# Causal masking moved from a matrix product to GpSimd and step rows, the V bias folded into the output bias, the order laid out anew

## The chip, the cores and the metric

One Trainium2 chip; the kernel runs on one of its cores. A core has TensorE (PE in the profile; PEld is its weight loads), VectorE (DVE), ScalarE (ACT), GpSimd (POOL) and the DMA queues, here issued by SyncE (SP). Times are device microseconds of one launch.

## The reference

Sixteen sequences of 512 positions and width 256 pass six residual steps: an FFN whose inputs and weights are rounded blockwise to FP4, a Mamba block (a scan over 512 positions), the FFN again, a LoRA mixture, causal attention with ALiBi, and the LoRA mixture again. The change touches the attention:

```
def _L1_attn_ref(x, Wq, bq, Wk, bk, Wv, bv, Wo, bo):
    B, S, D, H = (2, 512, 256, 16)
    HD = D // H
...
    v = (x @ Wv + bv).reshape(Bb, Ss, H, HD)
    scores = jnp.einsum('bthd,bshd->bhts', q, k) / jnp.sqrt(jnp.asarray(HD, x.dtype))
    alibi = _alibi_bias(Ss, Ss, x.dtype)
    causal = jnp.triu(jnp.ones((Ss, Ss), bool), 1)
    scores = scores + alibi[None]
    scores = jnp.where(causal[None, None], -jnp.inf, scores)
    attn = jax.nn.softmax(scores, axis=-1)
    out = jnp.einsum('bhts,bshd->bthd', attn, v).reshape(Bb, Ss, Dd)
    return out @ Wo + bo
```

## The kernel before

One sequence is one round (rounds are counted from 0). From one round's first `va` write to the next it is some 274 us (round 4 at 1857.7, round 5 at 2130.8). Four threads of work are woven into each other: the FFNs and the head of the Mamba block (`first`), the scan (`second`), LoRA, attention and LoRA (`third`), and the norms ahead of them (`ahead`). They work on different sequences at the same time. Each engine has one queue of instructions in program order. What stands next to what is set by tables of numbers (`PE_PLAN`, `DVE_PLAN`, `ACT_PLAN`, `POOL_PLAN`, `SP_PLAN`, one dictionary for each thread): each step of a thread yields a time of its own, the table replaces it by a due time, and `weave` emits the steps in order of due time. A table changes the order alone, never how long anything takes.

Scan: 16 steps a sequence, each in two halves. For each half DVE multiplies the input into a PSUM tile `u` (L1557), scans it with the decay into `state` (L1562), and POOL multiplies `state` by C (L728) so that PE can sum it (L1174). POOL's product of a half waits for the `u` of the half behind it. `state` has three slots, and a slot is loaded again when PE has summed it.

FFN: four tiles a sequence, twice. Tanh on ScalarE, products and rounding on DVE (L1474, L1477, L1373 to L1387), a rescaling on POOL (L712), transposes and products on PE (L1092, L1112, L1118).

Attention: 16 heads in four sets j of four heads g, 512 positions in four tiles t. Phase `s` computes scores with queries on the partitions (L1270), adds a mask on the diagonal block by a product of an identity with `mask_q` (L1275), and DVE takes the maxima (L1650). Phase `e` computes the scores again with keys on the partitions, less the maxima (L1272), adds `mask_k` in the same way (L1275), and ScalarE writes exponentials into `pt` (L979), one unit at a time: four units for t = 0 and t = 1, two for t = 2, one for t = 3, 11 a set. Scores go to the PSUM banks `pg` and `pu` in turn. Then the value products (L1295) multiply each head's part of `pt` with `va`, which has a column of ones for the sum. `pt` holds two groups (j, t). On PE the value products of a group stand behind the scores of the next group (`after_group`). `va` is written by DVE, product plus bias (L1612), from `pd` and `pg`.

## Time and profile before

| | |
|---|---|
| Median of 3 runs | 4930.08 us (4922.24 to 6492.46) |
| The profiled execution | 4930.1 us, of which the span is 4928.3 |
| Busy, share of the span | PE 80%, DVE 81%, ACT 48%, POOL 32% |
| Mean granted clock of TensorE | 0.89 |
| Instructions | 52598, of these 17452 matmuls and 1035 on POOL |

Busy shares are means over a start, a steady stretch and a tail with different limits. An idle time is put down to what came last before the instruction started. Matmul ends are modelled; the distance from one start to the next shows what a matmul takes of PE when others stand behind it.

### The profile page before, as it was taken

The numbers are of one execution on the slowest core, as the hardware profiler recorded it, in microseconds if no ns is written. First come the engines' busy times: TensorE is split into PE (matmuls) and PEld (weight loads), VectorE is DVE, ScalarE is ACT, GpSimd is POOL, SyncE is SP. The second block draws the span as 40 slices with busy tenths as digits, with TensorE's granted clock in tenths as the row PEclk, the third lists the DMA queues.
The fourth block names the chain that finished last, engine by engine and source line by source line (L and its number), as shares of the span: only waits on it lengthen the run. The fifth ranks groups of instructions, "written<-read, shape, count | busy, mean of one in ns | idle before, by whom it ended". The sixth has DMA issues, their size and how long they took to land.

```text
span 4928.3 us, 52598 instructions
## 1 busy us (share of the span) xinstructions
PE 3918.3 (80%) x17452; PEld 1986.8 (40%) x17452; DVE 3998.4 (81%) x5964; ACT 2373.6 (48%) x4341; POOL 1599.9 (32%) x1035
## 2 busy tenths in 40 slices
PE   4556678887879888888989888888889798786868
PEld 2212334443535353444435353434435353334343
DVE  6588889898989989898989899898989899683412
ACT  2334344655555554645555554546555555443322
POOL 0143433333333333333333333333333333332000
PEclk8677889998989999998989899999989999797866
DMA  1487667767686777777677777777676867772100
GB/s 56 118 180 174 154 170 174 186 153 182 152 180 171 161 176 169 178 170 176 158 181 174 156 178 158 177 174 190 154 178 152 181 166 164 180 160 61 38 28 22
DMA packets 241427, 753.30 MB, mean 153 GB/s; under 512 B 37650, under 2 KB 132659, under 8 KB 171524
## 3 DMA queue, kind: packets, MB, share of 16 engines
q1 hardware_dynamic: 241156, 749.95, 64.7%
q8 instruction: 138, 2.26, 0.2%
q14 instruction: 133, 1.09, 0.1%
HBM read 647.30 MB, written 101.71 MB: 152 GB/s over the span
## 4 chain that ended last, share of the span: by engine, by line
PE 46%; DVE 26%; ACT 11%; DMA 9%; issue 5%; SPq 2%; POOL 2%; DVEq 0%; ACTq 0%; POOLq 0%
PE m L1118 6%; DVE state L1562 6%; DMA state<-dtx_scratch 5%; PE m L1092 5%; DVE mt L1650 5%; DVE u L1557 3%; PE y L1174 3%; PE m L1131 2%; PE y L1184 2%; PE pd L1295 2%; DMA decay<-dt_scratch 2%; ACT shared L979 2%; DVE front L1474 1%; PE pd L1210 1%; DVE front L1477 1%
## 5 line engine op out<-in xcount | busy, mean ns | idle before, releaser
L728 POOL TENSOR_TENSOR state<-state,bc 128x1024 f32<-128x1024 f32 x512 | 1216.0, 2376 | 1786.1 <-DVE u L1557 1786.1
L1562 DVE TENSOR_TENSOR_SCAN state<-decay,u 128x1024 f32<-128x1024 f32 x512 | 1169.1, 2283 | 13.8 <-ACT decay L909 1.8
L909 ACT ACTIVATE decay<-decay,a_neg 128x511 f32<-128x511 f32 x1024 | 671.1, 712 | 280.4 <-DMA decay<-dt_scratch 280.2
L1092 PE MATMUL m<-w_gu,hats_m 128*128 128x480 f32 (+1 forms) x1536 | 722.8, 604 | 38.7 <-DVE front L1477 31.3
L1557 DVE TENSOR_TENSOR u<-state,bc 128x1024 f32<-128x1024 f32 x512 | 632.8, 1236 | 85.5 <-DMA state<-dtx_scratch 74.9
L712 POOL TENSOR_TENSOR front<-front,hsc_m 128x704 f32<-128x704 f32 x128 | 206.1, 1610 | 797.1 <-DVE front L1387 797.1
L1118 PE MATMUL m<-w_dn,front 128*128 128x256 f32 (+1 forms) x1536 | 419.4, 418 | 42.6 <-ACT front L846 42.2
L1092 PEld LDWEIGHTS m<-w_gu,hats_m 128*128 128x128 f32 x1536 | 298.4, 205 | 303.0 <-issue 225.8
L1174 PE MATMUL y<-state,sel 128*32 128x512 f32 x2048 | 307.4, 676 | 132.2 <-POOL state L728 130.9
L1131 PE MATMUL m<-hats_m,w_in 128*128 128x512 f32 x512 | 292.0, 712 | 145.4 <-DVE front L1516 92.8
L1118 PEld LDWEIGHTS m<-w_dn,front 128*128 128x128 f32 (+1 forms) x1536 | 289.1, 201 | 164.7 <-ACT front L846 85.7
L827 ACT ACTIVATE front<-m 128x240 f32<-128x240 f32 (+1 forms) x384 | 137.0, 361 | 307.2 <-PE m L1092 281.7
L1650 DVE TENSOR_REDUCE mt<-pu 128x1 f32<-128x384 f32 (+3 forms) x368 | 235.1, 639 | 42.3 <-PE pu L1275 38.9
L1650 DVE TENSOR_REDUCE mt<-pg 128x1 f32<-128x384 f32 (+3 forms) x336 | 212.8, 633 | 48.2 <-PE pg L1275 47.4
L979 ACT ACTIVATE shared<-pg 128x512 f32<-128x512 f32 (+1 forms) x384 | 215.1, 560 | 59.8 <-PE pg L1275 58.3
L850 ACT ACTIVATE xx<-m 128x256 f32<-128x256 f32 x128 | 49.1, 383 | 374.8 <-PE m L1119 374.8
L1131 PEld LDWEIGHTS m<-hats_m,w_in 128*128 128x128 f32 x512 | 105.7, 223 | 298.2 <-DVE front L1516 113.9
L979 ACT ACTIVATE shared<-pu 128x512 f32<-128x512 f32 (+1 forms) x320 | 177.3, 554 | 91.3 <-PE pu L1275 87.6
L1474 DVE SCALAR_TENSOR_TENSOR front<-front,m 128x240 f32<-128x240 f32 (+1 forms) x384 | 149.1, 388 | 66.6 <-ACT front L827 66.6
L1295 PE MATMUL pd<-shared,va 128*17 128x512 f32 (+3 forms) x2048 | 199.8, 459 | 1.9
L693 POOL TENSOR_SCALAR less_r<-mv_r 128x4 f32<-128x4 f32 x48 | 13.5, 282 | 560.9 <-DVE mv_r L1438 560.9
L1272 PE MATMUL pg<-shared,kh 105*128 105x128 bf16 (+3 forms) x640 | 147.7, 297 | 57.4 <-ACT shared L979 48.0
(259 smaller groups left out, 7051.8 us busy)
## 6 DMA issues: line engine op xcount, KB each, us to landing
decay<-dt_scratch SPq DMA_DIRECT2D x256, 1024.0 KB, 7.4
state<-dtx_scratch SPq DMA_DIRECT2D x256, 1024.0 KB, 11.6
qk_scratch<-shared SPq DMA_DIRECT2D x64, 384.0 KB, 3.1
shared<-qk_scratch SPq DMA_DIRECT2D x384, 64.0 KB
kh<-qk_scratch SPq DMA_DIRECT2D x384, 64.0 KB
xs_scratch<-front SPq DMA_DIRECT2D x16, 1024.0 KB, 5.8
dt_scratch<-front SPq DMA_DIRECT2D x256, 64.0 KB, 2.7
dtx_scratch<-hats_m SPq DMA_DIRECT2D x256, 64.0 KB, 1.9
```

Source lines behind the costliest of these rows:

```text
L712: eng.tensor_tensor(blocks(f.hq[:, t % 2, :]), blocks(f.xn[:, 0:I]), spread(f.hsc[:, t % 2, :], I // QB), ALU.mult).then_inc(f.pool.sem, f ...
L728: eng.tensor_tensor(st, st, bc[:, 1:2, :].to_broadcast([P, WIDE, L]), ALU.mult).then_inc(scan_pool.sem, scan_pool.step(f"c{r}{h}"))
L909: ins = eng.activation(d, d, ACT.Exp, scale=a_neg[:, g:g + 1])
L979: eng.activation(pt[:, slot:slot + n, 0:width], heads(f"e{j}{t}{g}", width, n), ACT.Exp).then_inc(att_act.sem, att_act.step(f"e{j}{t}{g}"))
L1092: mm = eng.matmul(f.bank(f"gu{t}{p}")[:, 0:2 * width], norm.hat_t[:, k, t * P:(t + 1) * P], w_gu[:, k, 2 * lo:2 * (lo + width)], start=(k ...
L1118: eng.matmul(down[:, 0:D], f.h_t[0:rows, m, :], w_dn[0:rows, m, :], start=(m == 0), stop=False)
L1131: mm = eng.matmul(bank[:, :], w_in[:, k, m * P:(m + 1) * P], norm.hat_t[:, k, :], start=(k == 0), stop=(k == KD - 1))
L1174: mm = eng.matmul(Y[32 * j:32 * (j + 1), :], sel[:, r % Q, :], state[:, slot, j * L:(j + 1) * L], start=False, stop=(r % Q == Q - 1), skip ...
L1295: eng.matmul(PD[32 * g:32 * g + HD + 1, t * P:L], va[:, t, j * G + g, :], pt[:, (t * G + g) % NPT, 0:L - t * P], start=(t == 0), stop=True ...
L1557: eng.tensor_tensor(u[:, :].rearrange("p (j l) -> p j l", j=WIDE), st.rearrange("p (j l) -> p j l", j=WIDE), bc[:, 0:1, :].to_broadcast([P ...
L1562: eng.tensor_tensor_scan(st, decay[:, n % ND, h * WIDE * L:(h + 1) * WIDE * L], u[:, :], 0.0, ALU.mult, ALU.add).then_inc(scan_dve.sem, sc ...
L1650: eng.tensor_reduce(mt[:, t, g:g + n], heads(f"s{j}{t}{g}", (t + 1) * P, n), AX.X, ALU.max, negate=True).then_inc(att_dve.sem, att_dve.ste ...
```

## The change

The mask product of phase `e` is taken out. In its place the score product of phase `e` gets 15 more rows in its contraction (105 rows become 120): row n of the queries' side is -1e30 for queries ahead of position 32 (n + 1), row n of the keys' side is one from that position on. A score is therefore masked when a multiple of 32 lies between query and key. What is left over, inside blocks of 32, is set to zero behind the exponential: a new instruction on POOL for each group (j, t), `affine_select` on the 128x4x128 elements of the diagonal block in `pt`, waits for the last exponential of the group, and the value products of all four heads wait for it instead of for their exponentials. There are 16 a round, 256 in all. Phase `s` keeps its mask.

The V bias is multiplied by Wo once, at setup, and added to the output bias; `va` is then a plain copy, which ScalarE makes instead of DVE. Setup gets one more group of products on PE with a copy on ScalarE, four small loads for the step rows, and loses the cast of `mask_k`.

All five plan tables are laid out anew, as is the distance `PERIOD` that they are repeated at. In the diff one row of a table stands for them.

```
-SROWS = MAXROW + 3
+STEP = 32
+STEPROW = MAXROW + 3
+SROWS = STEPROW + L // STEP - 1
...
-        PERIOD = 261.4610
+        PERIOD = 260.8583
...
-            {3: 662.9826, 27: 705.8361, 134: 913.8724},
+            {3: 666.7164, 27: 698.7656, 67.3: 788.3245, 69.5: 791.0211, 71.7: 792.7006, 73.9: 795.5432, 76.1: 806.0033, 78.3: 806.849,
...
-            load(bv[:, :], a["bv"].rearrange("(o d) -> o d", o=1).to_broadcast([P, D]))
-            load(bo[:, :], a["bo"].rearrange("(o d) -> o d", o=1).to_broadcast([P, D]))
+            load(bv[:, :], a["bv"].rearrange("(k p) -> p k", p=P))
+            load(bo[:, :], a["bo"].rearrange("(o d) -> o d", o=1))
...
+            for side, src in ((qh, "step_q"), (kh, "step_k")):
+                for b in range(2):
+                    load(side[STEPROW:SROWS, b, :, :].bitcast(I16), a[src].rearrange("s (o l) -> s o l", o=1).to_broadcast([SROWS - STEPROW, G, L]))
...
-                    eng.dma_start(kh[POS:SROWS, b, :, :].bitcast(I16), a["pos_k"][:, heads, :]).then_inc(qk_loaded[b], 16)
+                    eng.dma_start(kh[POS:STEPROW, b, :, :].bitcast(I16), a["pos_k"][:, heads, :]).then_inc(qk_loaded[b], 16)
...
+                for k in range(NG):
+                    w, j, t = kind(k)
+                    if w == "e":
+                        yield GROUP_AT(k) + 1.7
+                        eng.wait_ge(att_act.sem, att_act.after(r, f"e{j}{t}{units('e', t)[-1][0]}"))
+                        slot = t * G % NPT
+                        own = pt[:, slot:slot + G, 0:P]
+                        eng.affine_select(own, own, pattern=[[0, G], [1, P]], compare_op=ALU.is_ge, fill=0.0, base=0, channel_multiplier=-1
+                                          ).then_inc(att_pool.sem, att_pool.step(f"keep{j}{t}"))
...
+            n += 1
+            eng.wait_ge(set_pe, n + 1)
+            eng.activation(bo[0:1, :], RB[n % 4][0:1, 0:D], ACT.Copy).then_inc(set_act, 1)
...
-            assert n == 16
+            assert n == 17
...
+                for t in range(T):
+                    yield 19 + t
+                    if t == 0 and r:
+                        eng.wait_ge(att_pe.sem, att_pe.after(r - 1, f"p{J - 1}{T - 1}{G - 1}"))
+                    eng.wait_ge(att_pe.sem, att_pe.after(r, f"v{t}"))
+                    eng.activation(va[:, t, :, 0:HD], (PD, PG)[t % 2][:, 0:D].rearrange("p (h r) -> p h r", r=HD), ACT.Copy
+                                   ).then_inc(att_act.sem, att_act.step(f"v{t}"))
+
...
+            n += 1
+            free(n)
+            for k in range(KD):
+                eng.matmul(RB[n % 4][0:1, 0:D], bv[:, k:k + 1], w_o[:, k, :], start=(k == 0), stop=False)
+            eng.matmul(RB[n % 4][0:1, 0:D], ident[0:1, 0:1], bo[0:1, :], start=False, stop=True).then_inc(set_pe, 1)
...
-                        eng.wait_ge(att_dve.sem, att_dve.after(r, f"v{t - 2}"))
+                        eng.wait_ge(att_act.sem, att_act.after(r, f"v{t - 2}"))
...
-                            eng.matmul(out, kh[0:SROWS, b, g + h, t * P:(t + 1) * P], qh[0:SROWS, b, g + h, t * P:L],
+                            mm = eng.matmul(out, kh[0:SROWS, b, g + h, t * P:(t + 1) * P], qh[0:SROWS, b, g + h, t * P:L],
...
-                    first, mask = (t * P, mask_q) if w == "s" else (0, mask_k)
-                    eng.matmul(heads(event, width, n)[:, :, first:first + P], ident16[:, :],
-                               mask[:, :].rearrange("p (o l) -> p o l", o=1).to_broadcast([P, n, P]), start=False, stop=True, skip_group_check=True
-                               ).then_inc(att_pe.sem, att_pe.step(event))
+                    if w == "s":
+                        mm = eng.matmul(heads(event, width, n)[:, :, t * P:(t + 1) * P], ident16[:, :],
+                                        mask_q[:, :].rearrange("p (o l) -> p o l", o=1).to_broadcast([P, n, P]), start=False, stop=True, skip_group_check=True)
+                    mm.then_inc(att_pe.sem, att_pe.step(event))
...
+                    eng.wait_ge(att_pool.sem, att_pool.after(r, f"keep{j}{t}"))
...
-                        n = units("e", t)[0][1]
-                        eng.wait_ge(att_act.sem, att_act.after(r, f"e{j}{t}{g // n * n}"))
...
-                for t in range(T):
-                    yield 19 + t
-                    if t == 0 and r:
-
-                        eng.wait_ge(att_pe.sem, att_pe.after(r - 1, f"p{J - 1}{T - 1}{G - 1}"))
-                    eng.wait_ge(att_pe.sem, att_pe.after(r, f"v{t}"))
-                    eng.tensor_tensor(va[:, t, :, 0:HD], (PD, PG)[t % 2][:, 0:D].rearrange("p (h r) -> p h r", r=HD),
-                                      bv[:, :].rearrange("p (h r) -> p h r", r=HD), ALU.add).then_inc(att_dve.sem, att_dve.step(f"v{t}"))
-
...
+    first = np.arange(STEP, L, STEP)[:, None]
+
+    def bits(rows16):
+
+        return np.ascontiguousarray((rows16.astype(np.float32).view(np.uint32) >> 16).astype(np.uint16))
+
...
+        "step_q": bits(np.where(np.arange(L)[None, :] < first, MASKED, 0.0)),
+        "step_k": bits(np.where(np.arange(L)[None, :] >= first, 1.0, 0.0)),
...
-        "mask_k": np.where(k < q, np.float32(MASKED), np.float32(0.0)),
```

POOL, beside the last two thirds of sequence 7's scan. `state` rows are the C products of the scan, `front` rows the rescalings of the FFN. Before:

```order
L712 TENSOR_TENSOR front<-front,hsc_m 128x704 [waits ffn_pe_m,ffn_dve_m]
L728 TENSOR_TENSOR state<-state,bc 128x1024 [waits scan_dve] x3
L712 TENSOR_TENSOR front<-front,hsc_m 128x704 [waits ffn_pe_m,ffn_dve_m]
L728 TENSOR_TENSOR state<-state,bc 128x1024 [waits scan_dve] x4
L712 TENSOR_TENSOR front<-front,hsc_m 128x704 [waits ffn_pe_m,ffn_dve_m]
L728 TENSOR_TENSOR state<-state,bc 128x1024 [waits scan_dve] x7
```

Now, the same place (L734 is L728 of before, L718 is L712):

```order
L734 TENSOR_TENSOR state<-state,bc 128x1024 [waits scan_dve]
L718 TENSOR_TENSOR front<-front,hsc_m 128x704 [waits ffn_pe_m,ffn_dve_m]
L749 AFFINE_SELECT shared<-shared 128x4x128 [waits att_act]
L734 TENSOR_TENSOR state<-state,bc 128x1024 [waits scan_dve]
L749 AFFINE_SELECT shared<-shared 128x4x128 [waits att_act] x2
L734 TENSOR_TENSOR state<-state,bc 128x1024 [waits scan_dve]
L749 AFFINE_SELECT shared<-shared 128x4x128 [waits att_act] x2
L734 TENSOR_TENSOR state<-state,bc 128x1024 [waits scan_dve] x2
L749 AFFINE_SELECT shared<-shared 128x4x128 [waits att_act] x3
L734 TENSOR_TENSOR state<-state,bc 128x1024 [waits scan_dve] x3
L718 TENSOR_TENSOR front<-front,hsc_m 128x704 [waits ffn_pe_m,ffn_dve_m]
L734 TENSOR_TENSOR state<-state,bc 128x1024 [waits scan_dve]
```

Eight selects stand in one half of the round's attention, behind and ahead of single C products.

PE, round 3, phase `e` of the first head set, from the value products of tile 0 on. Before:

```order
L1295 MATMUL pd<-shared,va 17x512 [waits att_act] x4
L1272 MATMUL pg<-shared,kh 128x256 [waits att_act]
L1272 MATMUL pg<-shared,kh 128x256
L1275 MATMUL pg<-mask_k,ident 128x2x128
L1272 MATMUL pu<-shared,kh 128x256 [waits att_act]
L1272 MATMUL pu<-shared,kh 128x256
L1275 MATMUL pu<-mask_k,ident 128x2x128
L1295 MATMUL pd<-shared,va 17x384 [waits att_act] x4
L1272 MATMUL pg<-shared,kh 128x128 [waits att_act]
L1272 MATMUL pg<-shared,kh 128x128 x3
L1275 MATMUL pg<-mask_k,ident 128x512
```

Now (L1303 is L1272, L1325 is L1295):

```order
L1325 MATMUL pd<-shared,va 17x512 [waits att_pool]
L1325 MATMUL pd<-shared,va 17x512 x3
L1303 MATMUL pg<-shared,kh 128x256 [waits att_act]
L1303 MATMUL pg<-shared,kh 128x256
L1303 MATMUL pu<-shared,kh 128x256 [waits att_act]
L1303 MATMUL pu<-shared,kh 128x256
L1325 MATMUL pd<-shared,va 17x384 [waits att_pool]
L1325 MATMUL pd<-shared,va 17x384 x3
L1303 MATMUL pg<-shared,kh 128x128 [waits att_act]
L1303 MATMUL pg<-shared,kh 128x128 x3
L1123 MATMUL m<-w_gu,hats_m 128x448 [waits ffn_dve_m]
```

The sequence is the same without the mask rows; the value products wait for POOL's semaphore in place of ScalarE's.

DVE before, at the first `va` product of round 6 (`u` and `state` belong to the scan, `skip` is its gate):

```order
L1540 TENSOR_TENSOR skip<-y,gate 128x512 [waits gate_loaded0,scan_pe]
L1612 TENSOR_TENSOR va<-pd,bv 128x16x16 [waits att_pe]
L1557 TENSOR_TENSOR u<-state,bc 128x1024 [waits scan_dve,state_loaded1]
L1562 SCALAR_TENSOR_TENSOR state<-decay,u 128x1024 [waits scan_act,scan_dve]
L1434 BN_STATS stats_m<-xx 128x6 [waits ffn_act_m]
```

ScalarE now, at the copies of the same round (L927 is L909, L810 evacuates the FFN's transposed input, L845 is the tanh):

```order
L927 ACTIVATE decay<-decay,a_neg 128x511
L974 ACTIVATE va<-pd 128x16x16 [waits att_pe]
L810 ACTIVATE hats_m<-m 128x512 [waits dt_saved1,gz_saved1,gz_saved0,ffn_pe_m,dt_saved0,xs_saved]
L810 ACTIVATE hats_m<-m 128x512 [waits ffn_pe_m]
L845 ACTIVATE front<-m 128x240 [waits ffn_dve_m,ffn_pe_m]
L974 ACTIVATE va<-pg 128x16x16 [waits att_pe]
L974 ACTIVATE va<-pd 128x16x16 [waits att_pe]
```

DVE loses four rows a round, ScalarE gets them between evacuations of the FFN.

## Rows read from the trace of the kernel before

**Rows 1.** Page, part 4: the chain that ended last, by engine and by line.

```profile
PE 46%; DVE 26%; ACT 11%; DMA 9%; issue 5%; SPq 2%; POOL 2%; DVEq 0%; ACTq 0%; POOLq 0%
PE m L1118 6%; DVE state L1562 6%; DMA state<-dtx_scratch 5%; PE m L1092 5%; DVE mt L1650 5%; DVE u L1557 3%; PE y L1174 3%; PE m L1131 2%; PE y L1184 2%; PE pd L1295 2%; DMA decay<-dt_scratch 2%; ACT shared L979 2%; DVE front L1474 1%; PE pd L1210 1%; DVE front L1477 1%
```

**Rows 2.** Windows: length, busy PE, PEld, DVE, ACT, POOL, clock, DMA; steady stretch, tail.

```profile
1034.00:4047.00 3013.00, 2563.26 (x11969) 1312.82 (x11968) 2706.49 (x4048) 1615.71 (x2960) 1093.49 (x705) 0.94 0.73 170
4480.00:4928.00 448.00, 339.28 (x1446) 183.17 (x1444) 122.89 (x313) 127.22 (x237) 24.81 (x38) 0.74 0.09 26
```

**Rows 3.** Groups by form: count, busy us, mean ns, idle before.

```profile
L1275 PE MATMUL pg<-mask_k,ident 128*128 128x128 bf16 x256 | 57.9, 226 | 0.0
...
L850 ACT ACTIVATE xx<-m 128x256 f32<-128x256 f32 x128 | 49.1, 383 | 374.8 <-PE m L1119 374.8
...
L1275 PE MATMUL pg<-mask_k,ident 128*128 128x512 bf16 x64 | 24.9, 389 | 0.0
...
L1275 PE MATMUL pg<-mask_k,ident 128*128 128x256 bf16 x64 | 18.9, 295 | 0.0
...
L1612 DVE TENSOR_TENSOR va<-pd,bv 128x256 f32<-128x256 f32 x32 | 13.5, 421 | 72.9 <-PE pd L1242 72.9
```

**Rows 4.** Timeline, round 1: a mask product and the product behind it, twice.

```profile
1083.70 0.38 PE L1275 MATMUL pg<-mask_k,ident 128*128 128x512 bf16 x1
...
1083.92 1.66 PE L1092 MATMUL m<-w_gu,hats_m 128*128 128x448 f32 x4
...
1087.97 0.38 PE L1272 MATMUL pu<-shared,kh 105*128 105x512 bf16 x1
...
1088.19 0.22 PE L1275 MATMUL pu<-mask_k,ident 128*128 128x128 bf16 x1
...
1088.25 0.38 PE L1272 MATMUL pg<-shared,kh 105*128 105x512 bf16 x1
```

**Rows 5.** Timeline, round 1: last exponential of a group, value products behind it.

```profile
1096.60 0.48 ACT L979 ACTIVATE shared<-pg 128x384 f32<-128x384 f32 x1
...
1097.95 0.84 PE L1295 MATMUL pd<-shared,va 128*17 128x384 f32 x8
1098.22 0.59 ACT L979 ACTIVATE shared<-pu 128x512 f32<-128x512 f32 x1
...
1099.27 0.63 PE L1295 MATMUL pd<-shared,va 128*17 128x256 f32 x8
...
1099.37 0.60 ACT L979 ACTIVATE shared<-pg 128x512 f32<-128x512 f32 x1 [0.56 <-PE pg L1275]
...
1100.37 0.41 PE L1295 MATMUL pd<-shared,va 128*17 128x128 f32 x8
```

**Rows 6.** Waits in the steady stretch: total us, times, longest.

```profile
DVE va L1612 <- PE pd L1242: 6.5, 11, 0.6
...
PE y L1174 <- POOL state L728: 44.3, 11, 5.4
```

**Rows 7.** Single lines: count, then ns as min/median/max.

```profile
L688 POOL MEMSET va<- x1: 995/995/995, 1.3 to 1.3; 128x1088 f32 x1
...
L712 POOL TENSOR_TENSOR front<-front,hsc_m x128: 1385/1389/2306, 82.7 to 4657.9; 128x704 f32<-128x704 f32 x128
...
L728 POOL TENSOR_TENSOR state<-state,bc x512: 2339/2352/3422, 217.3 to 4481.0; 128x1024 f32<-128x1024 f32 x171
...
L1557 DVE TENSOR_TENSOR u<-state,bc x512: 1206/1227/2589, 208.8 to 4477.3; 128x1024 f32<-128x1024 f32 x171
...
L1562 DVE TENSOR_TENSOR_SCAN state<-decay,u x512: 2253/2286/2290, 213.6 to 4478.6; 128x1024 f32<-128x1024 f32 x171
```

**Rows 8.** Timeline, round 6: a rescaling on POOL beside a product on DVE.

```profile
2450.05 1.23 DVE L1557 TENSOR_TENSOR u<-state,bc 128x1024 f32<-128x1024 f32 x1
2450.21 2.31 POOL L712 TENSOR_TENSOR front<-front,hsc_m 128x704 f32<-128x704 f32 x1 [1.75 <-DVE front L1387]
```

**Rows 9.** Timeline, end of setup: what DVE's first statistics waited for.

```profile
52.06 1.40 DVE L1434 BATCH_NORM_STATS2 stats_m<-xx 128x6 f32<-128x256 f32 x4 [5.23 <-ACT vec L779]
```

More of the change, by code:

```diff
@@ L118, in build @@
         w_lb = sb("w_lb", [E * R + 1, D])
-        bv = sb("bv", [P, D])
-        bo = sb("bo", [P, D])
+        bv = sb("bv", [P, KD])
+        bo = sb("bo", [1, D])
         rb = sb("rb", [P, E])
```

17 lines of the change are left out of this document (8 added, 9 removed), and 204 rows, old and new, of tables (ACT_PLAN, DVE_PLAN, PE_PLAN, POOL_PLAN).

## The prediction

> **What bounds the kernel now.** I read the chain that ended last first, since busy shares alone don't tell what a microsecond is worth: PE holds 46% of it, DVE 26%, ScalarE 11%, DMA 9%, POOL 2% [rows 1]. The reader is to see that no engine holds it alone, and that neither the mask product nor the `va` product is among its lines. Then the steady stretch: over 3013 us, eleven rounds, DVE is busy 90%, PE 85%, ScalarE 54% and POOL 36%, at a mean granted clock of 0.94; in the tail of 448 us the same engines have 27%, 76%, 28% and 6%, and the clock is 0.74 [rows 2]. So in the steady stretch a microsecond of DVE is worth most of itself (I take three quarters), one of PE about its share of the chain (46%), and one of ScalarE or POOL nothing, as long as nobody waits for it. The question is whether somebody now will.
>
> **The mask products go from PE.** There are 44 a round: per head set eight of 128 columns, two of 256 and one of 512, which is 512, 128 and 64 in all (one bank's forms stand in [rows 3]). Their means of 226, 295 and 389 ns overlap their neighbours. What one takes of PE is the distance to the start behind it: 0.06 us for 128 columns (1088.19 to 1088.25), 0.22 us for 512 (1083.70 to 1083.92) [rows 4]; for 256 I take 0.11 between them. 512 x 0.06 + 128 x 0.11 + 64 x 0.22 = 59 us. With the chain's share of 46% that is 27 us. The bounds are nothing, where ScalarE paces the scores anyway, and the whole 59. The score product itself keeps its columns and grows from 105 to 120 rows of contraction. No row shows a length that depends on rows at equal columns, so I take nothing for it.
>
> **The V product goes from DVE to ScalarE.** 64 x 0.421 us are 27 us of DVE [rows 3]. In the stretch DVE also stood 6.5 us in eleven rounds ahead of it [rows 6], which makes 9 us in sixteen; the 72.9 us of the whole run [rows 3] lie mostly in the start and the tail, where DVE has time. Together 36 us of DVE. ScalarE gets 64 copies, for which the nearest row is a copy of the same 128x256 from PSUM at 383 ns [rows 3]: 25 us on an engine that is idle 46% of the stretch. The copy waits for PE's product, and behind it on ScalarE stand the evacuation of the FFN's transposed input and the first tanh, for which PE and DVE wait. That it costs nothing rests on PE having made the product by then; if it is late, the wait of 0.6 us that DVE had at most [rows 6] is ScalarE's, 64 x 0.6 = 38 us at the very worst, and I leave it at nothing because it was 0.6 at the longest there. The bias product stays one row of the output product. Setup gets three small products and a copy in the line that DVE's first statistics wait for [rows 9]: 1 us.
>
> **How long a select takes.** The trace has none. From below, a write alone of 1088 elements took 995 ns, which makes 0.47 us for 512; from above, the product of two inputs of 1024 elements took 2352, half of which is 1.18 us [rows 7]. A select reads one input and writes, which stands between the two: 0.8 us. Page "GPSIMD Engine Reference" of the Trainium skill, section "Performance versus the Vector engine", gives 769 ns for 512 elements in the best one-input loop; no run here shows it, and an estimate by it would leave the sum where it is.
>
> **The value products wait for the select.** This is the term against the change. On PE they stand right behind the scores of the next group, and the new order keeps that. In one set of round 1 the last exponential of tile 1 ended at 1097.08, and its value products began at 1097.95: a gap of 0.87 us. For tile 2 it is 1098.81 to 1099.27, 0.46 us; for tile 3 1099.97 to 1100.37, 0.40 us [rows 5]. Tile 0 has other work between. A select of 0.8 us fits into the first, and outlasts the others by 0.34 and 0.40. Over 64 sets that is 47 us of new waiting on PE (5 us at 0.47, 116 at 1.18), at 46% some 22 us (2 to 53). What is queued behind: the next scores, hence the next exponentials, and the FFN's products.
>
> On top of it comes POOL's own queue. POOL is busy 36% of the stretch [rows 2], chiefly with C products of 2.35 us [rows 7]. Were a select to come at a random moment, 128 groups with a short gap x 0.36 x half of 2.35 us give 54 us on PE, 25 us at its share. The tables lay selects behind single C products, so I take half, 12 us; the bounds are 0 and 25, and the rival below goes past them.
>
> **The port.** A rescaling that started on POOL at 2450.21, while DVE multiplied two SBUF tiles until 2451.28, took 2.31 us [rows 8] where the median is 1.389, so it stood still until then; the other way round, `u` took up to 2.589 us where its median is 1.227 [rows 7]. An instruction of DVE with two inputs in SBUF and one of POOL that reads SBUF exclude each other. Today this hardly ever costs DVE anything, because the C product waits for `u` and then runs beside the scan (2352 and 2286 ns [rows 7]), whose other input is in PSUM. A select has no such place. DVE starts 512 `u` products and 3 x 128 rounding products of the FFN with two such inputs, in the 4270 us from the first `u` to the last [rows 7]: 0.21 a microsecond. 256 selects of 0.8 us meet 43 of them and hold each 0.4 us: 17 us of DVE (0 to 205, if each select held DVE for its whole length). DVE thus gains 36 - 17 = 19 us, worth 14.
>
> This is where a rule of the Trainium skill speaks against the change: "SBUF — State Buffer", section "Who interferes with whom", says that whichever of the two starts first has the shared port for its whole instruction, and the other fully blocks. The trace agrees, with the 2.31 and 2.589 us above. If DVE were only slowed a little, the port term would be near zero and the sum 4911; by the rule it stands as worked out.
>
> **The sum.** 4930.1 us is the profiled execution, of which the span is 4928.3, and the median of the three runs is 4930.08, the same number. 4930 - 27 (masks) - 14 (DVE) + 22 (select ahead of the values) + 12 (select behind a C product) + 1 (setup) = **4924 us**. Gains and costs are of one size. The new tables as such I take at nothing: rows on one queue show no stall that they plainly remove, and they can as well add one.
>
> **The rivals.**
>
> First, ScalarE paces phase `e`. With the mask gone the next unit's scores come 0.06 us earlier but wait for the bank that ScalarE frees, whose exponentials of 0.48 to 0.60 us are far longer than scores [rows 4, 5]. Then the masks give nothing, and the costs stay: 4924 + 27 = 4951. Against it speaks that much of PE's work there is other threads', which move up at once. This is also the case in which the change doesn't do what it says.
>
> Second, slower: POOL becomes a link between ScalarE and the scan. Behind a select on POOL stand C products directly, four in the half round that the order shows, nine in a whole one. If the exponentials come late, the select starts late, and the C product behind it is pushed past the scan beside which it ran; its 2352 ns leave no margin within 2286 [rows 7]. The next product of two SBUF inputs on DVE then waits for it. 9 x 16 x 0.8 us are 115 us, at three quarters 86. PE waits for C products already, 44.3 us in the stretch [rows 6], 64 in sixteen rounds, and that would double: 29 us. 4924 + 86 + 29 = 5039. It decides from the point where a select is still waiting or running as the `u` ahead of its C product ends. The rule named above is what makes it expensive. For it speaks that one order has to hold three engines together; against it, that POOL is idle almost two thirds of the time.
>
> Third, faster: PE and DVE are both wholly on the path in turn, selects take 0.47 us and find POOL free. 4930 - 59 - 36 + 2 + 1 = 4838. The chain's 46% and 26% speak against both at once.
>
> **How the numbers follow.** The forecast has 0.44, the pacing by ScalarE 0.24, the slower case 0.18, the faster one 0.10, and 0.04 remain for what I haven't thought of. The likeliest, 4924, has a range of its own from 4880 to 4975 by the bounds of the select. The whole range, 4840 to 5030, reaches from the faster case to the slower one and leaves a tenth out on either side. Two per cent, which is about what a measurement of this kernel tells from no change, is 99 us: faster than 4831 needs more than the third rival, 0.07; slower than 5029 is about half of the second, with some of the unforeseen, 0.12; within it 0.81.
>
> **What would show it.** A select near 0.8 us, and a wait of PE ahead of the value products for it of 45 to 100 us in all, where ScalarE's exponentials released them before. `u` products above 1.3 us more often than now, and a sum of DVE's lengthened instructions near 17 us. PE waiting for C products not much above 64 us in all; if it is twice that, the second rival holds. DVE's busy time down by 27 us less what the port adds. A round of the stretch within 1.5 us of its present 274. The prediction fails if the select takes over 1.2 us, if the C products leave the scan's side, or if the new tables remove or make a stall of several microseconds a round, which no row of before can tell.

## The result, and the profile after

The changed kernel takes 4954.8 us (median of 6 runs) where the kernel before took 4922.2 beside it on the same chip: a ratio of 1.0077, 95% interval 1.0054 to 1.0099. That is some 38 us slower, within two per cent and inside the range, but on the other side of the forecast's 6 us of gain. (Each ratio here is to the kernel before, run in the same session, and leaves disturbed runs out; by the medians the change is 33 us slower, and the two ways of reckoning differ by up to some 7 us below as well. A difference of two ratios carries an interval of about 0.2 to 0.35%, 10 to 17 us, on either side.) The profiled execution has a span of 4950.7 us.

The page after, parts 1 and 4, then the groups of the select, the value products and the transposes behind the rescaling:

```profile
PE 3917.0 (79%) x16725; PEld 1980.4 (40%) x16754; DVE 3999.3 (81%) x5899; ACT 2390.4 (48%) x4406; POOL 1785.6 (36%) x1291
...
PE 43%; DVE 24%; ACT 13%; DMA 7%; POOL 6%; issue 5%; SPq 2%; another core or an unknown queue 0%; ACTq 0%; DVEq 0%; POOLq 0%
...
L749 POOL TENSOR_SCALAR_AFFINE_SELECT shared<-shared 128x512 f32<-128x512 f32 x256 | 195.1, 766 | 404.8 <-ACT shared L1005 403.7
...
L1325 PE MATMUL pd<-shared,va 128*17 128x512 f32 (+3 forms) x2048 | 206.4, 479 | 79.2 <-POOL shared L749 78.9
...
L1143 PE MATMUL m<-ident,front 128*128 128x128 f32 (+1 forms) x768 | 146.3, 315 | 104.2 <-POOL front L718 77.3
```

POOL has gone from 2% to 6% of the chain [rows 1]. The windows of the changed kernel over the same steady stretch, and over its tail (columns as in [rows 2]):

```profile
1034.00:4047.00 3013.00, 2548.07 (x11269) 1294.77 (x11288) 2658.64 (x3929) 1596.21 (x2946) 1201.14 (x866) 0.90 0.73 168
4533.00:4950.00 417.00, 305.49 (x1326) 166.43 (x1324) 121.33 (x305) 127.21 (x243) 46.47 (x70) 0.77 0.09 28
```

Fewer of DVE's instructions fit into the same 3013 us, 3929 for 4048: 44 of the difference are the V products that went to ScalarE, the other 75 are work that did not get done. PE, DVE and ScalarE are each busy for less of the stretch than before, POOL alone for more. From the start of round 3's scan to round 14's, a round takes 279.0 us where it took 273.8, and the last scan starts at 4533.0, 54 us later than before [rows 7]. The tail behind it gives 32 of these back. Where PE waits in the stretch (total us, times, longest):

```profile
PE pd L1325 <- POOL shared L749: 61.9, 29, 5.0
PE pd L1361 <- ACT hats_r L1016: 55.5, 11, 5.0
PE m L1143 <- POOL front L718: 47.4, 21, 5.0
PE pg L1301 <- DVE hats_r L1659: 38.6, 11, 5.0
```

Only the first has anything to do with a select. All four have one longer wait in each of the eleven rounds, 3.4 to 5.0 us for the first three and 2.3 to 5.0 us for the fourth; the rest of their counts is short. The kernel before had two of that length, for other things: the C products' [rows 6], and 57.7 us in eleven waits of its projection (L1131) for VectorE's step on `front` (L1516). A third, the same projection for L1531, had 29.4 us in eleven waits of 1.6 to 3.6 us. The new tables took those away and made these four. Two of the long ones in the timeline of one round. First, POOL's third rescaling (L718) behind a third C product that had to wait for `u`:

```profile
2503.46 2.35 POOL L734 TENSOR_TENSOR state<-state,bc 128x1024 f32<-128x1024 f32 x1 [5.87 <-DVE u L1587]
...
2508.14 2.34 POOL L734 TENSOR_TENSOR state<-state,bc 128x1024 f32<-128x1024 f32 x1 [2.34 <-DVE u L1587]
2510.44 1.39 POOL L718 TENSOR_TENSOR front<-front,hsc_m 128x704 f32<-128x704 f32 x1
...
2511.88 1.11 PE L1143 MATMUL m<-ident,front 128*128 128x128 f32 x4 [4.07 <-POOL front L718]
```

Second, the last two exponentials of head group 3 behind a softplus block on ScalarE (L902, L907, two table loads), with the select behind them and the value products behind that:

```profile
2572.89 1.28 ACT L907 ACT_TABLE_LOAD   x1
2574.18 1.15 ACT L907 ACTIVATE front<-front 128x512 f32<-128x512 f32 x2
...
2575.35 1.28 ACT L1005 ACT_TABLE_LOAD   x1
2576.64 0.60 ACT L1005 ACTIVATE shared<-pu 128x512 f32<-128x512 f32 x1
...
2577.14 0.59 ACT L1005 ACTIVATE shared<-pg 128x512 f32<-128x512 f32 x1
2577.31 2.01 POOL L749 TENSOR_SCALAR_AFFINE_SELECT shared<-shared 128x512 f32<-128x512 f32 x2 [7.22 <-ACT shared L1005]
2578.34 1.67 PE L1325 MATMUL pd<-shared,va 128*17 128x256 f32 x16 [5.03 <-POOL shared L749]
```

The wait is booked on the select, but 3.6 of the 5 us are ScalarE's: without selects (`no_select`, below) the same value products wait 39.2 us in eleven times, 3.6 at the longest, for the exponentials alone. A wait's name is its last link.

PE is not the only engine that waits. DVE, with 24% of the chain, has as its largest wait in the stretch one that the kernel before did not have: its scan (L1592) stands once a round, 4.3 to 5.4 us, for the decay that ScalarE computes. Before, the scan waited 1.8 us for it in the whole run.

```profile
DVE state L1592 <- ACT decay L927: 56.7, 11, 5.4
```

Some 14 us behind the timeline above one can see where it comes from. ScalarE's copy of the second half of the attended rows (L1016) stands behind another softplus block, and PE waits for it; ScalarE then waits for PE's output products, of which L1363 is the last, to write `xx` (L1020), and the decay stands behind that:

```profile
2592.86 2.07 PE L1361 MATMUL pd<-w_o,hats_r 128*128 128x256 f32 x4 [5.05 <-ACT hats_r L1016]
...
2601.28 0.60 ACT L1020 ACTIVATE xx<-pd 128x512 f32<-128x512 f32 x1 [8.47 <-PE pd L1363]
2601.89 1.28 ACT L927 ACT_TABLE_LOAD   x1
...
2604.62 2.29 DVE L1592 TENSOR_TENSOR_SCAN state<-decay,u 128x1024 f32<-128x1024 f32 x1 [5.44 <-ACT decay L927]
```

### The profile page after: what moved, and what is told of

It is laid out like the page before. It is cut to its first block, busy times and chain, and to the rows that moved or that the text cites. A ratio compares the mean times of both kernels' runs of the same rounds, so it can differ in the third digit from the quotient of the medians.

```text
span 4950.7 us, 51433 instructions
## 1 busy us (share of the span) xinstructions
PE 3917.0 (79%) x16725; PEld 1980.4 (40%) x16754; DVE 3999.3 (81%) x5899; ACT 2390.4 (48%) x4406; POOL 1785.6 (36%) x1291
## 4 chain that ended last, share of the span: by engine, by line
PE 43%; DVE 24%; ACT 13%; DMA 7%; POOL 6%; issue 5%; SPq 2%; another core or an unknown queue 0%; ACTq 0%; DVEq 0%; POOLq 0%
PE m L1149 7%; PE m L1123 6%; DMA state<-dtx_scratch 6%; DVE state L1592 5%; PE m L1162 3%; POOL state L734 3%; DVE mt L1671 3%; DVE u L1587 3%; PE y L1205 2%; PE pd L1325 2%; PE m L1143 2%; PE m L1175 1%; PE y L1215 1%; PE m L1183 1%; PE m L1150 1%
## 5 line engine op out<-in xcount | busy, mean ns | idle before, releaser
L734 POOL TENSOR_TENSOR state<-state,bc 128x1024 f32<-128x1024 f32 x512 | 1215.0, 2374 | 1429.6 <-DVE u L1587 1429.2
L1592 DVE TENSOR_TENSOR_SCAN state<-decay,u 128x1024 f32<-128x1024 f32 x512 | 1167.8, 2281 | 91.6 <-ACT decay L927 80.6
L1123 PE MATMUL m<-w_gu,hats_m 128*128 128x480 f32 (+1 forms) x1536 | 699.8, 589 | 58.6 <-DVE front L1507 39.7
L927 ACT ACTIVATE decay<-decay,a_neg 128x511 f32<-128x511 f32 x1024 | 675.2, 712 | 71.7 <-DMA decay<-dt_scratch 71.1
L1587 DVE TENSOR_TENSOR u<-state,bc 128x1024 f32<-128x1024 f32 x512 | 653.1, 1276 | 69.5 <-DMA state<-dtx_scratch 60.2
L718 POOL TENSOR_TENSOR front<-front,hsc_m 128x704 f32<-128x704 f32 x128 | 206.8, 1616 | 783.8 <-DVE front L1417 783.8
L1149 PE MATMUL m<-w_dn,front 128*128 128x256 f32 (+1 forms) x1536 | 438.5, 433 | 34.8 <-ACT front L864 34.8
L1123 PEld LDWEIGHTS m<-w_gu,hats_m 128*128 128x128 f32 x1536 | 285.7, 197 | 331.3 <-issue 217.6
L1205 PE MATMUL y<-state,sel 128*32 128x512 f32 x2048 | 315.4, 692 | 76.1 <-POOL state L734 75.8
L1149 PEld LDWEIGHTS m<-w_dn,front 128*128 128x128 f32 (+1 forms) x1536 | 307.1, 212 | 159.7 <-ACT front L864 68.4
L749 POOL TENSOR_SCALAR_AFFINE_SELECT shared<-shared 128x512 f32<-128x512 f32 x256 | 195.1, 766 | 404.8 <-ACT shared L1005 403.7
L1162 PE MATMUL m<-hats_m,w_in 128*128 128x512 f32 x512 | 277.3, 670 | 56.9 <-DVE front L1546 31.4
L845 ACT ACTIVATE front<-m 128x240 f32<-128x240 f32 (+1 forms) x384 | 134.6, 362 | 326.1 <-PE m L1123 307.5
L1671 DVE TENSOR_REDUCE mt<-pu 128x1 f32<-128x384 f32 (+3 forms) x368 | 234.3, 637 | 67.8 <-PE pu L1306 66.6
L1671 DVE TENSOR_REDUCE mt<-pg 128x1 f32<-128x384 f32 (+3 forms) x336 | 212.7, 633 | 76.0 <-PE pg L1306 73.9
L1325 PE MATMUL pd<-shared,va 128*17 128x512 f32 (+3 forms) x2048 | 206.4, 479 | 79.2 <-POOL shared L749 78.9
L864 ACT ACTIVATE front<-m 128x512 f32<-128x512 f32 (+1 forms) x256 | 121.5, 488 | 300.2 <-PE m L1143 299.3
L1301 PE MATMUL pg<-kh,shared 102*128 102x512 bf16 (+3 forms) x448 | 141.4, 358 | 112.2 <-DVE hats_r L1659 53.2
L1143 PE MATMUL m<-ident,front 128*128 128x128 f32 (+1 forms) x768 | 146.3, 315 | 104.2 <-POOL front L718 77.3
```

Of the source, the lines that this page charges most:

```text
L734: eng.tensor_tensor(st, st, bc[:, 1:2, :].to_broadcast([P, WIDE, L]), ALU.mult).then_inc(scan_pool.sem, scan_pool.step(f"c{r}{h}"))
L927: ins = eng.activation(d, d, ACT.Exp, scale=a_neg[:, g:g + 1])
L1123: mm = eng.matmul(f.bank(f"gu{t}{p}")[:, 0:2 * width], norm.hat_t[:, k, t * P:(t + 1) * P], w_gu[:, k, 2 * lo:2 * (lo + width)], start=(k ...
L1143: mm = eng.transpose(dst[0:rows, (m - lo) * P:(m - lo + 1) * P], f.hq[:, t % 2, m * P:m * P + rows], ident[:, :])
L1149: eng.matmul(down[:, 0:D], f.h_t[0:rows, m, :], w_dn[0:rows, m, :], start=(m == 0), stop=False)
L1162: mm = eng.matmul(bank[:, :], w_in[:, k, m * P:(m + 1) * P], norm.hat_t[:, k, :], start=(k == 0), stop=(k == KD - 1))
```

## The experiments

Theories: **A**, the select costs (its wait, or its queue and port); **B**, the new tables cost by themselves; **C**, what the change removes gives nothing; **D**, the TensorE clock, whose mean in the stretch fell from 0.94 to 0.90. The expectations were written with letters of their own: their A and B are these, their C is D here, and their D, D2, E and F are on the waits that the new tables made (D and D2: these cost the time; E and F: something else does); A2 and A3 are on selects in the old order.

### Taking the change apart

`no_select` leaves the selects out of the changed kernel, and with them the mask inside blocks of 32 (the select's own lines go too and are not shown here):

```diff
...
-                    eng.wait_ge(att_pool.sem, att_pool.after(r, f"keep{j}{t}"))
+                        n = units("e", t)[0][1]
+                        eng.wait_ge(att_act.sem, att_act.after(r, f"e{j}{t}{g // n * n}"))
```

> The changed kernel with its new tables, the 16 selects of a round left out, and the value products waiting for their exponentials as in the kernel before. Left out: the causal mask inside each block of 32 (the step rows stay). Theory A (the select costs: TensorE waited 158 us for it over the run in rows of after, and 47 to 62 us of that in the steady stretch, ahead of value products): 40 to 60 us come off, 4900 to 4920 us. Theory B (the new tables cost, the select next to nothing): within 12 us of the changed kernel, 4940 to 4965. Theory C (TensorE's half clock costs: 34.1 us of a round at 1.2 GHz before, 57.1 after): the time follows the half clock, so 57 us a round stay if the time stays, about 34 if it comes down.

It took 4932.9 us against 4925.5, ratio 1.0019 (1.0004 to 1.0033). The select is worth 0.58% in this order, 28 us (22 by the medians), and a loss of 9 stays without any select. That lies between the two expectations: neither the select alone nor the tables alone. The mean clock in the stretch stays at 0.90.

`old_order_no_select` also leaves selects out, and has the period and all five tables of before; ScalarE's table gets its copies of V, and one step of its FFN is put behind the last of them:

```diff
-        PERIOD = 260.8583
+        PERIOD = 261.4610
...
+             ... 43: 749.6872, 44: 753.4148, 45: 758.0, 46: 759.064
```

> The order of the kernel before, without mask products, with V copied by ScalarE and without selects; left out is the causal mask inside each block of 32. It is the change's gain alone. The prediction's terms -27 (masks) and -14 (VectorE) give 4880 to 4890 us. The rival that masks give nothing because ScalarE paces the exponentials gives 4905 to 4925 (only VectorE's part). Theory C, that a lighter TensorE loses its clock: half clock rises over 45 us a round and the time stays within 10 us of before.

4891.8 us, ratio 0.9938 (0.9921 to 0.9955). This is the removals alone: 30 us, at the edge of what the prediction's terms gave (4880 to 4890) and clear of the rival. **C** falls and **B** holds: between it and `no_select` lies only the order, and that is 0.81%, 40 us. Its stretch and its PE waits:

```profile
1034.00:4047.00 3013.00, 2550.02 (x11539) 1302.57 (x11562) 2715.31 (x4030) 1631.17 (x3023) 1101.03 (x711) 0.94 0.73 171
```

```profile
PE m L1150 <- DVE front L1535: 60.4, 11, 6.6
PE y L1193 <- POOL state L732: 47.1, 18, 4.8
```

These are the two of the kernel before. The four of the new tables are not there. The clock is 0.94 without any mask product, so it is not the lighter TensorE that lowers it.

`masks_back` has the new tables, no selects, and the mask products (the lines that they replace are not shown):

```diff
...
+                    first, mask = (t * P, mask_q) if w == "s" else (0, mask_k)
+                    eng.matmul(heads(event, width, n)[:, :, first:first + P], ident16[:, :],
```

> The new tables with the mask products of the kernel before and no selects; V stays on ScalarE. It computes the reference and is the kernel before in the new order, but for V. Theory B (the new tables are worse by themselves): 4950 to 4980 us. Theory A (the select costs): 4915 to 4935, and no_select 15 to 30 us below it if mask products cost what the prediction says, the same if they lie where TensorE waits anyway. Theory C: mask products keep the clock up, half clock near 34 us a round, and this kernel is no slower than no_select.

4969.1 us, ratio 1.0101 (1.0082 to 1.0119), as **B** had it: a kernel that computes what the kernel before does, in the new order, is 1% slower. So mask products are worth 0.82%, 40 us, in the new order, and with them the clock is 0.90 all the same. The expectation that masks keep the clock up fell.

`v_only2` is the kernel before with V's bias folded and V copied by ScalarE, masks kept, and with the 15 step rows in the scores of phase `e`:

> The order of the kernel before with its mask products and no selects; only V's bias is folded and V copied by ScalarE. With old_order_no_select (4891.8 us) it splits the 34 us between the two removals. The prediction had 27 for the masks and 14 for VectorE: 4911 to 4918 us. The rival of masks that give nothing: 4892 to 4900. If VectorE's part gives nothing: 4920 to 4928.

4915.5 us against 4923.6, ratio 0.9993 (0.9980 to 1.0005): 3 us, between 10 gained and 2 lost; by the medians 8. The step rows are in it and cost nothing that the rows show: score products of 128 and 256 columns take 219 and 283 ns in the median with 120 rows of contraction as with 105. The masks in the old order then are 0.9993 to 0.9938, 27 us.

### The select: wait, or queue and port

`sel_unwaited2` keeps each select at its place on POOL, on a buffer of its own in bfloat16, and PE does not wait for it:

```diff
-                        slot = t * G % NPT
-                        own = pt[:, slot:slot + G, 0:P]
+                        own = spare[:, :, :]
```

> The changed kernel with each select done on a buffer of its own, as wide in elements (in bfloat16) and at the same place of GpSimd's queue, and the value products waiting for the exponentials alone; left out is the causal mask inside blocks of 32. It keeps GpSimd's queue and the use of the port and takes away TensorE's wait. If the 22 us between no_select and the changed kernel are TensorE's waits: 4930 to 4938 us. If they are the queue and VectorE's lengthened instructions (u 25.6 us in the profile of after, 5.3 before): 4948 to 4957.

4930.3 us, ratio 1.0026 (1.0010 to 1.0042), beside 1.0019 without selects and 1.0077 for the whole. DVE is busy 3998.9 us here against 3978.5 in `no_select`, so the port does take its 20 us of DVE. The selects themselves take as long as in the changed kernel (637 ns in the median). Of the time they cost 3 us by the ratios, which the intervals don't tell from nothing. What costs is PE's wait: some 25 us, with an interval of about 13 on either side.

### The select in the old order

`old_order` is the whole change in the old order, selects at their exponentials' due times (the C products and rescalings get new due times on POOL as well, but stand in their old sequence, in this kernel and the next):

```diff
+ 67.3: 789.2502, 69.5: 789.2502, 71.7: 789.8581, 73.9: 800.4886, 76.1: 803.7448, 78.3: 805.5983, 80.5: 805.5983, 82.7: 808.2884
```

> All of the change's code with the due times and the period of the kernel before. Only what the old tables have no place for is placed: a select right behind its last exponential's due time (or just ahead of its value products' where that is earlier), the C products of GpSimd in their old order but with due times at which they really run, and ScalarE's four copies of V between 749.7 and 759.1. Theory B (the new tables cost): 4925 to 4940 us, a round near 274 us, half clock near 34 us of it. Theory A (the select costs, whatever the order): 4955 to 4975. A theory in between, that the new tables were laid out for the select and are the better home of it: above 4975, since the value products wait for a select in places that left no room for one.

5232.2 us, ratio 1.0633 (1.0612 to 1.0653). Of the three expectations the last holds, above 4975, but none had a loss of this size. PE waits 208.0 us in the stretch for selects, 11.1 at the longest. The timeline shows a select whose exponential ended at 3209.4:

```profile
3208.76 3.31 POOL L729 TENSOR_TENSOR state<-state,bc 128x1024 f32<-128x1024 f32 x1
...
3208.80 0.60 ACT L1000 ACTIVATE shared<-pg 128x512 f32<-128x512 f32 x1 [0.85 <-PE pg L1298]
...
3212.04 1.37 POOL L713 TENSOR_TENSOR front<-front,hsc_m 128x704 f32<-128x704 f32 x1
3213.38 2.33 POOL L729 TENSOR_TENSOR state<-state,bc 128x1024 f32<-128x1024 f32 x1
3215.67 0.62 POOL L744 TENSOR_SCALAR_AFFINE_SELECT shared<-shared 128x512 f32<-128x512 f32 x1
...
3216.35 0.63 PE L1320 MATMUL pd<-shared,va 128*17 128x128 f32 x8 [6.34 <-POOL shared L744]
```

Three of POOL's instructions, the first already running, stand between an exponential and its select of 0.62 us. `sel_placed2` puts each select behind the instruction of POOL that runs just before its exponential ends, never behind the next:

```diff
+ 67.3: 785.8345, 69.5: 793.5806, 71.7: 793.6006, 73.9: 793.6046, 76.1: 793.6086, 78.3: 807.502, 80.5: 807.506, 82.7: 807.51
```

> The code of the change in the order of the kernel before, as old_order, with one thing different: each of the 16 selects stands on GpSimd's queue behind the C product or rescaling that runs just before its last exponential ends in the trace of old_order_no_select, never behind the next one, which waits for a later u. old_order put four of them (those of head groups and blocks 0-3, 1-3, 3-1 and 3-2) behind a C product that waited for VectorE: value products stood 7 to 14 us behind their exponentials there. Theory A2 (a select costs little where nothing stands ahead of it on its queue): 4891.8 plus 16 times 16 selects of which about 7 in 16 are waited for by TensorE for some 0.8 us at the chain's share of 46%, 40 us at most: 4895 to 4935 us, a round of 272 to 275 us. Theory A3 (the old order has no room for selects wherever they stand, since its value products follow their exponentials at 0.8 us): above 4960 us.

4960.0 us, ratio 1.0088 (1.0070 to 1.0105). 270 us of the loss were the places. The upper theory, over 4960, is met at its edge all the same: even well placed, selects cost 0.0150 here, 74 us, over two and a half times what they cost in the new tables. There the value products stand later: without selects they begin 2.1 us behind their group's last exponential in the median of 256, in the old order 1.5 (`no_select` and `old_order_no_select`). PE waits for the selects 86 times in the stretch, 2.1 us at the longest:

```profile
PE pd L1320 <- POOL shared L744: 70.0, 86, 2.1
```

Without selects the same products wait 3.0 us here and 39.2 in the new tables, so selects add 67 us of PE's waiting here and 23 there. So the old order has no room for selects at either of the two placements tried. A new order had a reason; what was wrong with this one is something else.

### The waits of the new tables

`two_swaps2` is the changed kernel with two due times altered, so that the rescaling and the two exponentials shown above stand one place earlier:

```diff
-             171: 83.6406, 174.5: 84.6584, 178: 91.2209, 180: 94.8161, 182.8: 95.9772, 185.6: 105.404, 188.4: 111.0732, 196: 119.2867,
+             171: 83.6406, 174.5: 84.6584, 178: 91.2209, 180: 94.8161, 182.8: 96.03, 185.6: 105.404, 188.4: 111.0732, 196: 119.2867,
-             105.5: 295.9269, 110: 292.2047, 116.5: 259.0081, 121: 306.6825, 127.5: 318.6463, 132: 302.2726, 138.5: 331.128, 143: 343.8342,
+             105.5: 295.9269, 110: 292.2047, 116.5: 297.78, 121: 306.6825, 127.5: 318.6463, 132: 302.2726, 138.5: 331.128, 143: 343.8342,
```

> The changed kernel with two due times altered. On GpSimd the third rescaling of a round goes ahead of the third of three C products instead of behind it (TensorE waited 3.9 to 4.1 us for it each round); on ScalarE the last two exponentials of head group 3 go ahead of a softplus block of two table loads and five activations (TensorE waited 3.6 to 5.0 us for them). Each wait stood just ahead of a stretch of 10 to 27 us at 1.2 GHz. Theory D (these waits are what the new tables cost, and the low clock behind them more than the waits themselves): half clock falls from 57 to under 42 us a round, a round from 279.0 to 275 or less, the time to 4900 to 4935 us. Theory E (the new tables are slower in many small places, or the chain runs elsewhere): half clock may fall, the time stays within 10 us of 4955.

4912.2 us, ratio 0.9977 (0.9961 to 0.9994): two numbers are worth 1.0%, 49 us. The waits on L718 are gone, and those on the select are down to 6.7 us. Two others stay, and one came up behind the exponentials (L1354). VectorE's wait for the decay also stays, 44.9 us in eleven times:

```profile
PE pd L1361 <- ACT hats_r L1016: 55.5, 11, 5.1
...
PE pg L1301 <- DVE hats_r L1659: 44.0, 11, 5.1
PE pg L1354 <- DVE hats_r L1659: 43.1, 11, 4.3
```

The round is 276.4 us and the mean clock still 0.90. The time is what the expectation's D had, but its half on the clock is not borne out, and the round stayed above its 275. One swap at a time:

> The changed kernel with one due time altered, the first of the two of two_swaps2 (4912.2 us): on GpSimd the third rescaling of a round goes ahead of the third of three C products. TensorE waited for it 3.9 to 4.1 us a round, 47.4 us with another in the steady stretch. If the 43 us that both swaps gave follow the length of the waits removed (about 4.0 and 5.0 us a round): 4932 to 4940. If this one does it all, since VectorE's FFN work and with it the scan hangs on the rescaling: 4912 to 4920. If the other does: 4948 to 4958.

> The changed kernel with the other due time of two_swaps2 altered alone: on ScalarE the last two exponentials of head group 3 go ahead of the softplus block. By length of the waits: 4930 to 4938 us. If it does it all, since it ends the attention of a round: 4912 to 4920. If nothing: 4948 to 4958.

4928.8 (ratio 1.0009, 0.9994 to 1.0025) and 4932.5 (0.9999, 0.9982 to 1.0015). They give 33 and 38 us by the ratios, for 44 and 54 us less of these two waits in the eleven rounds, 64 and 79 in sixteen: about half. Together they give less than their sum by the ratios, 49 for 71. Behind a wait removed others appear in both (VectorE's maxima, L1671, 22.5 to 53.2 us in the stretch with the first; L1354, 43.0, with the second); that this is the whole reason is not shown.

`five_swaps` adds three moves: ScalarE's copy of the attended rows' second half goes ahead of a softplus block (two due times, 124 and 127), VectorE's division of head group 3 ahead of another, and that of head group 1 ahead of a `u` product that waits for a transfer.

```diff
-             64.7: 786.9946, 65.2: 778.5311, 65.25: 787.5548, 78.5: 807.0251, 83.5: 811.882, 85.7: 786.0166, 86.7: 813.1735, 87.3: 818.2792,
+             64.7: 786.9946, 65.2: 778.5311, 65.25: 787.5548, 78.5: 807.0251, 83.5: 811.882, 85.7: 786.0166, 86.7: 813.1735, 87.3: 816.0,
-             98.9: 826.7092, 99.4: 848.5309, 99.9: 834.5147, 100.4: 843.93, 100.45: 849.634, 113.7: 874.5101, 122.5: 895.6999, 131: 914.7684,
+             98.9: 826.7092, 99.4: 848.5309, 99.9: 834.5147, 100.4: 843.93, 100.45: 849.634, 113.7: 874.5101, 122.5: 887.7, 131: 914.7684,
-             115.3: 878.5892, 116.5: 846.5035, 120.5: 886.0083, 123.5: 889.1439, 124: 899.1019, 127: 893.248, 129: 905.049, 136: 920.3944,
+             115.3: 878.5892, 116.5: 846.5035, 120.5: 886.0083, 123.5: 889.1439, 124: 891.0, 127: 899.1019, 129: 905.049, 136: 920.3944,
```

> two_swaps2 and three more due times, each for a wait of TensorE that stood once a round in its steady stretch and that the kernel before had not: the copy of the attended rows' second half by ScalarE goes ahead of a softplus block (TensorE waited 5.0 to 5.1 us for it), and VectorE's division of head group 3 ahead of a softplus block (4.3) and of head group 1 ahead of a u product that waits for a transfer (5.0). 43 us came from taking away about 8 us of waits a round (130 over the run), a third of their sum; 14.4 us a round here, 230 over the run, give 75 at that rate, less what VectorE's scan and union of 246 us a round allow. Theory D2 (waits of a few us that the new tables made are their cost): 4850 to 4895 us, a round of 270 to 273 us. Theory F (the round is by now held by VectorE, 246.3 of 276.4 us busy): 4900 to 4915.

4866.8 us, ratio 0.9863 (0.9837 to 0.9888): faster than both kernels, with selects, and 2.1% below the change as it was made, 105 us. A round is 272.2 us. VectorE's wait for the decay is gone as well, from 80.6 us in the changed kernel's whole run to 13.1; the copy moved is the first link of the timeline that led to it, but no run moves the copy alone.

```profile
1034.00:4047.00 3013.00, 2585.50 (x11533) 1317.68 (x11553) 2734.28 (x4036) 1635.36 (x3018) 1221.31 (x886) 0.91 0.75 172
```

```profile
PE pu L1301 <- DVE mt L1671: 52.3, 78, 2.8
PE y L1205 <- POOL state L734: 41.9, 15, 4.7
```

The second is the kernel before's wait for C products, back again: fewer and shorter waits are left, not none.

> five_swaps without selects, value products waiting for their exponentials; left out is the causal mask inside blocks of 32. Beside five_swaps it gives the select's price where its surroundings wait for nothing longer: with two_swaps2 TensorE waited 6.7 us for selects in the steady stretch, where the changed kernel had 61.9. If the price is that wait: within 8 us of five_swaps. If the select costs by what it adds between an exponential and its value products anywhere: 15 to 30 us below it.

4855.9 us, ratio 0.9855 (0.9832 to 0.9877). Against `five_swaps` that is 4 us by the ratios and 11 by the medians, which the intervals don't tell from nothing nor from 15. It is less than the 28 of the select among the unrepaired waits, though by little more than the four intervals together leave open.

## Why the prediction failed, step by step

In ratios, from before to after: V 0.9993, masks 0.9938, tables 1.0019, selects 1.0077.

- **What failed** is the one term without a row: "The new tables as such I take at nothing". They cost 40 us, more than the whole removals gave. The text had named the case (tables that make "a stall of several microseconds a round, which no row of before can tell") and gave it neither a price nor a chance of its own. Four such stalls of PE it was, and one of VectorE's scan, for two and a shorter third taken away, and a round of 279.0 us where 274 within 1.5 was forecast. Each of the four came from an instruction standing late on its queue: the rescaling and the division of head group 1 behind one that waited for another engine or a transfer, the exponentials and the copy behind a softplus block. With these moved ahead, and one more division that came up behind them, the same tables gave 105 us back (`five_swaps`). The rows of before couldn't price them, but the order of the changed kernel shows them as questions: what stands ahead of it on this queue, and what does that wait for.
- **Masks, -27.** Measured 27 in the old order, 40 in the new. The term was right, and the first rival, that they give nothing, is refuted in both orders. Its spread over all rounds was not: from the profile of `v_only2` to that of `old_order_no_select`, the last scan starts 18 us earlier (4486.0 to 4468.4), and another 16 us come from the tail of some 430.
- **V, -14.** Measured 3, and at most 10 (8 by the medians). DVE's busy time fell by 15 us (3998.4 to 3983.4 in `v_only2`) instead of 27, because 17 instead of 4 `u` products were lengthened there. The copy on ScalarE took 379 and 384 ns for the 383 of its nearest row [rows 3].
- **How long a select takes.** 0.637 us in the median, 0.766 in the mean, between the bounds and below the 0.8 taken. The trace shows two kinds: 637 undisturbed, and longer ones up to 1691 (59 of 256 were lengthened, by 33 us in sum; the others took 626 to 647). The 769 ns for 512 elements in the best loop, from "GPSIMD Engine Reference" of the Trainium skill, section "Performance versus the Vector engine", is near the mean only by these longer ones: an undisturbed select here took 0.13 us less.
- **Select ahead of the value products, and behind a C product, 22 + 12.** Measured some 25 for both. The 22 rested on the gaps of one set of round 1, and on the new order keeping them; it lengthened them (2.1 us for 1.5 in the median). PE's wait, foretold as 45 to 100 us, was 78.9 in the whole run. But its make-up was different: in the stretch 29 waits, of which eleven were the one behind the softplus block. Where the values had other work ahead of them, the wait was near nothing.
- **The port, 17 us of DVE.** `sel_unwaited2` against `no_select` has 20 more, so the size was right. Its worth, three quarters of it, came out at 3 us by the ratios, too little for the intervals to tell. DVE's busy share of 90% did not mean that its every microsecond counts; that it has slack because it waits elsewhere in each round, 56.7 us for the decay alone, is an argument and no run shows it.
- **The second rival**, POOL as a link between ScalarE and the scan, did not come: a C product takes 2352 ns in the median as before, what DVE waited for ahead of `u` was a transfer (60.2 of 69.5 us), and PE's wait for them fell from 130.9 to 75.8 us over the run (in the stretch from 44.3 to 4.9). What it described, an instruction of POOL pushed back by one queued ahead of it, did happen, to the rescaling and with C products as the ones in front.
- **The clock (theory D).** In each of the eleven rounds the granted clock of the changed kernel fell to 1.2 GHz within some 2 us of the end of PE's wait for the select behind the softplus block, and stayed there for 20 to 27 us, over PE's next wait (L1361): from 2576.0 to 2603.6 its mean is 0.51. The kernel before has 10 to 21 us at this level at the same place of its rounds (2551.5 to 2568.6: 0.50). With a mean of 0.90, a fifth of the stretch is at the lower level, with 0.94 an eighth. The lower mean comes with the new tables, with or without masks and selects, and also with `old_order` (0.90), whose waits for selects are up to 11.1 us. Yet the time doesn't follow it: `two_swaps2` gained 49 us at 0.90, `five_swaps` is the fastest at 0.91, and `sel_placed2` has 0.93 and is no faster than the changed kernel. What the lower clock costs by itself no run isolated; it stays open.

Not isolated either: how much of the tables' remaining difference (`five_no_select` is 41 us faster than `old_order_no_select` by the ratios) is a better order as such, and how much the moves of `five_swaps`, some of whose waits had nothing to do with masks, V or selects.

## What to carry to other kernels

When a change comes with a new static order, the order is a term of its own, here the largest, and is worth a run alone: old code in the new order, or new code in the old. After it, list the waits of every engine that has a large share of the chain, by count and longest: one that stands as often as there are rounds, at 3 to 5 us, is worth following back, past the instruction that it is booked on, to what stands ahead on that queue. Here five such moves, of one or two due times each, were worth 105 us; one of the waits came up only when others were gone. A cheap instruction put between two engines costs what stands ahead of it on its queue; the same 0.63 us select was worth 4 to 11, 28, 74 or 340 us by its place.

## What the runs showed of the hardware

A select over 128 partitions x 512 fp32 elements takes 626 to 647 ns on GpSimd when undisturbed (637 in the median, and 637 in bfloat16 in `sel_unwaited2`), and up to 1691 beside DVE's products of two SBUF inputs: 31 of the 59 lengthened ones met a `u` product, the others products on `front`. Beside them 57 `u` products took over 1.3 us, where the kernel before had 4. The 20 us by which DVE's busy time grew cost 3 us of the total, not told from nothing. A change between ScalarE's functions shows as an ACT_TABLE_LOAD of 1.28 us, once into a softplus block and once out of it. A score product takes the same time with 120 rows of contraction as with 105 (219 ns at 128 columns, 283 at 256).
